# Softmax by head on ScalarE ahead of the transposes, and the layer norms on GpSimd, in an audio tower kernel

## The reference

```python
h = tokens(x)                       # 93 overlapping patches of 16 frames a sequence, 128 numbers each, + bias
h = h + attention(layernorm(h))     # a second layer norm with gamma and beta inside
h = h + experts(layernorm(h))
# attention, 8 heads of 64; q, k, v = projection, then 3 taps along the sequence
sim  = q @ k.T * 64 ** -0.5 - slope[head] * abs(i - j);  sim[j > i] = -max
out  = softmax(sim) @ v;  return out @ wout.T
# experts: 2 of 16 experts for each token; each expert's mean of silu(x @ w1.T) over its tokens goes through w2
```

## Time and profile before

| what | value |
|---|---|
| median of 3 runs | 793.95 us (793.44 to 796.95) |
| profiled execution | 798.25 us, span of its instructions 796.4 us |
| PE busy | 742.8 us, 93% of the span |
| DVE, ACT, POOL busy | 618.8, 471.6, 375.1 us (78%, 59%, 47%) |
| mean granted TensorE clock | 0.965 of 2.4 GHz |
| attention part (first to last row maximum) | 73.0 to 631.3 us |

### The profile page before, as it was taken

One profiled execution on the slowest core, in us unless ns is written; L12 is line 12 of the kernel. 1 busy time (PEld: TensorE's weight loads), 2 busy tenths in 40 slices (PEclk: granted clock), 3 DMA queues, 4 the chain that ended last, 5 costly groups with the idle time before them and its releaser, 6 DMA issues.

```text
span 796.4 us, 20698 instructions
## 1 busy us (share of the span) xinstructions
PE 742.8 (93%) x6770; PEld 691.7 (87%) x6770; DVE 618.8 (78%) x1645; ACT 471.6 (59%) x998; POOL 375.1 (47%) x390
## 2 busy tenths in 40 slices
PE   5678999999999999999999999998998878999986
PEld 4568999999999999999999999997877777999984
DVE  2255878888888888888888888889988648888875
ACT  3444556666566656666655656565543456899960
POOL 3642243666564655655565646554362455122200
PEclk9887999999999999999999999999999968999996
DMA  5421123331221111222111221102124012122205
GB/s 184 140 67 51 40 80 101 127 103 51 57 65 53 49 49 49 53 58 59 49 49 50 68 53 51 50 11 71 33 75 170 19 45 67 51 66 63 62 22 154
DMA packets 44269, 53.97 MB, mean 68 GB/s; under 512 B 13651, under 2 KB 31251, under 8 KB 43696
## 3 DMA queue, kind: packets, MB, share of 16 engines
q1 hardware_dynamic: 30048, 38.84, 16.9%
q0 software_dynamic: 12544, 12.87, 5.8%
q10 hardware_dynamic: 1616, 1.48, 0.6%
HBM read 42.69 MB, written 10.26 MB: 66 GB/s over the span
## 4 chain that ended last, share of the span: by engine, by line
PE 75%; DVE 12%; ACT 4%; issue 3%; DMA 2%; POOL 2%; DVEq 1%; ACTq 0%; SPq 0%
PE psTP L452 10%; PE psSO L590 9%; PE psTP L453 8%; PE psTP L454 8%; PE psSO L672 7%; PE psSO L612 6%; PE psSO L538 4%; PE psTP L524 3%; PE psTP L557 3%; PE psSO L710 3%; PE psTP L710 3%; DMA x_raw<-in_x 2%; PE psTP L635 2%; PE psSO L607 2%; DVE qkv L975 2%
## 5 line engine op out<-in xcount | busy, mean ns | idle before, releaser
L1329 POOL DMA_INDIRECT expert_rows<-hn,slot x128 | 167.6, 1309 | 66.6 <-DVE slot L1177 34.3
L1262 POOL TENSOR_TENSOR x_lo<-x_raw,x_hi 128x752 fp32r<-128x752 f32 x64 | 114.9, 1796 | 142.6 <-ACT x_hi L780 142.6
L975 DVE SCALAR_TENSOR_TENSOR qkv<-psTP,taps,qkv 128x368 f32<-128x368 f32 x192 | 113.9, 593 | 74.6 <-ACT qkv L788 73.2
L788 ACT ACTIVATE qkv<-psTP,taps 128x372 f32<-128x372 f32 x192 | 108.8, 567 | 89.0 <-PE psTP L454 88.7
L978 DVE SCALAR_TENSOR_TENSOR qkv<-psTP,taps,qkv 128x364 f32<-128x364 f32 x192 | 114.6, 597 | 6.8
L452 PE MATMUL psTP<-x_hi,wtok_hi 128*128 128x376 f32 x256 | 94.5, 369 | 13.7 <-DVE wtok_lo L963 9.0
L590 PEld LDWEIGHTS psSO<-vrow,probT 93*93 93x93 f32 x1024 | 94.6, 164 | 4.5 <-ACT probT L830 3.5
L590 PE MATMUL psSO<-vrow,probT 93*93 93x65 f32 x1024 | 95.0, 247 | 1.8 <-DVE resid L1110 0.8
L453 PE MATMUL psTP<-x_lo,wtok_hi 128*128 128x376 f32 x256 | 88.1, 344 | 0.0
L454 PE MATMUL psTP<-x_hi,wtok_lo 128*128 128x376 f32 x256 | 87.8, 343 | 0.0
L452 PE MATMUL psTP<-xnT_hi,wqkv_hi 128*128 128x372 f32 x192 | 77.8, 405 | 9.1 <-DVE qkv L978 5.0
(11 more groups left out here) (193 smaller groups left out, 1577.3 us busy)
## 6 DMA issues: line engine op xcount, KB each, us to landing
x_raw<-in_x SPq DMA_DIRECT2D x64, 376.0 KB, 3.2
w1s<-in_w POOLq DMA_DIRECT2D x8, 512.0 KB, 4.8
w<-in_w SPq DMA_DIRECT2D x4, 1024.0 KB, 6.9
out<-resid SPq DMA_DIRECT2D x16, 160.0 KB, 2.5
xsE<-expert_rows SPq DMA_DIRECT2D x36, 64.0 KB, 2.1
xs<-expert_rows SPq DMA_DIRECT2D x36, 64.0 KB, 1.8
xs<-expert_rows POOLq DMA_DIRECT2D x36, 64.0 KB, 2.1
expert_rows<-hn,slot POOLq DMA_INDIRECT x128, 3.5
```

Of the source, the lines that this page charges most:

```text
L788: nc.scalar.activation(qkv[u][:, k, :, :], psP[(k + 1) % 2][:, 0:GT].rearrange("p (b n) -> p b n", n=NT), ACT.Copy, scale=taps[:, k, 2:3]) ...
L975: nc.vector.scalar_tensor_tensor(dst[:, :, 1:NT], src[:, :, 0:NT - 1], taps[:, k, 1:2], dst[:, :, 1:NT], ALU.mult, ALU.add).then_inc(tap1_ ...
L1262: nc.gpsimd.tensor_tensor(x_lo[u][:, 0:PIECE], x_raw[u][:, :], x_hi[u][:, 0:PIECE].bitcast(F32), ALU.subtract)\
L1329: nc.gpsimd.indirect_dma_start(rows, bass.IndirectOffsetOnAxis(slot[1 - u][:, c:c + 1], 0), hn[1 - u][:, c % GB, :], None)\
```

## The change

The softmax is turned round. Before, the row maximum was subtracted, the scores were transposed, the exponential was taken on the way out of PSUM, and the sum and the division came behind the product with the values. Now:

- The scores are made negative (taps of q scaled by -1/8, bias with the other sign), DVE takes their minimum, and ACT's exponential reads them from PSUM with scale -1 and the minimum as bias, which is a number per partition and head: so there is one instruction for each head, 8 of 93x93, in two halves (exponentials(0) and (1)), with the copy of v between them.
- DVE sums prob, takes the reciprocal, and multiplies: three instructions behind a wait for both halves (exp_done), between the first conv and the other two of a step.
- PE transposes the finished probabilities into psPT (parts of psO's first bank and of psV), ACT copies them to probT, and the product has vrow as weights (93x64) and probT as moving data, so that its output is already transposed; head pairs lie on the two halves of the columns. The transposes of attn and the array attn are gone, and so are the ones in vrow.
- PE's order is: scores, first projection, transposes of prob, one patch tap, transposes of v, one tap, the product, second projection, a tap, a tap, third projection, output projection. ACT starts a step with the first tap2, the copy to resid and x_hi.
- Both layer norms' last part, ACT's four Identity instructions, becomes two instructions of GpSimd (93x512, product and sum), ahead of x_lo in its queue.

```diff
--- before.py
+++ after.py
-        vrow = [sb(f"vrow{u}", [NT, H, DH + 1]) for u in range(2)]
-        rmax = sb("rmax", [NT, 2, 4])
-        shifted = sb("shifted", [NT, 2, 4, NT])
+        vrow = [sb(f"vrow{u}", [NT, H, DH]) for u in range(2)]
+        rmin = sb("rmin", [NT, 2, 4])
+        prob = sb("prob", [NT, 2, 4, NT])
+        den = sb("den", [NT, 2, 4])
         probT = sb("probT", [NT, 2, 4, NT])
         rden = sb("rden", [NT, 2, 4])
-        attn = sb("attn", [NT, H * DH])
...
-        psTot = psO[:, 0, 264:264 + E]
+        psTot = psO[:, 1, 0:E]
         psRT = psV[:, 384:384 + NT]
+        psPT = [psO[:NT, 0, 0:GT], psV[:NT, 0:GT]]
...
+            def scores(t, u, s, n):
+
+                if s == 0:
+                    wait(pe, conv_done, (t - 3) * NBLK + 2 * QB)
+                    if isinstance(t, int) and t == 3:
+                        pe.wait_ge(bias_cast, 4)
+                        pe.wait_ge(attn_w_in, 16 * 4)
+                wait(pe, exp_done, n * 2)
+                wait(pe, rden_done, n)
+                for a in range(2):
+                    nc.tensor.matmul(psS[:NT, a, 0:4 * NT], ident16[:NT, :NT], bias[:, a, :],
+                                     start=True, stop=False, skip_group_check=True)
+                for hh in range(4):
+                    for a in range(2):
+                        lo = 64 * a
+                        mm = nc.tensor.matmul(psS[:NT, a, hh * NT:(hh + 1) * NT],
+                                              qkv[1 - u][lo:lo + 64, hh, s, :], qkv[1 - u][lo:lo + 64, QB + hh, s, :],
+                                              start=False, stop=True, skip_group_check=True)
+                mm.then_inc(s_mm, 1)
+
+            def turn_prob(t, f, s, n):
+
+                pe.wait_ge(prob_ready, n)
+                wait(pe, res_add, n - 1)
+                pe.wait_ge(v_evac, n)
+                if f.scat and s == 1:
+                    wait(pe, rwT_evac, t - 4)
+                for a in range(2):
+                    for hh in range(4):
+                        mm = nc.tensor.transpose(psPT[a][:, hh * NT:(hh + 1) * NT], prob[:, a, hh, :], ident[:NT, :NT])
+                    mm.then_inc(p_tr, 1)
+
+            def turn_values(t, u, f, s, n):
+
+                if s == 0:
+                    pe.wait_ge(conv_done, (t - 2) * NBLK)
+                wait(pe, p_evac, n * 2)
+                for j in range(QB):
+                    mm = nc.tensor.transpose(psV[:NT, j * 128:(j + 1) * 128],
+                                             qkv[1 - u][:, 2 * QB + j, s, :], ident[:, :])
+                mm.then_inc(v_tr, 1)
+
+            def weigh(s, n):
+
+                pe.wait_ge(p_evac, n * 2)
+                pe.wait_ge(v_evac, n)
+                for hh in range(4):
+                    for a in range(2):
+                        mm = nc.tensor.matmul(psO[64 * a:64 * a + 64, 0, hh * NT:(hh + 1) * NT],
+                                              vrow[(s + 1) % 2][:, 2 * hh + a, :], probT[:, a, hh, :],
+                                              start=True, stop=True)
+                mm.then_inc(pv_mm, 1)
...
+                    if f.attn:
+                        scores(t, u, s, n)
+                    if f.proj:
+                        proj(t, u, f, 3 * s)
                     if prev:
-
-                        pe.wait_ge(shift_done, n)
-                        for a in range(2):
-                            for hh in range(4):
-                                mm = nc.tensor.transpose(psS[:NT, a, hh * NT:(hh + 1) * NT], shifted[:, a, hh, :],
-                                                         ident[:NT, :NT])
-                            mm.then_inc(p_tr, 1)
+                        turn_prob(t, f, s, n)
...
+                        turn_values(t, u, f, s, n)
...
+                        weigh(s, n)
...
-                        pe.wait_ge(norm_done, n)
-                        for j in range(QB):
-                            mm = nc.tensor.transpose(psV[:, j * NT:(j + 1) * NT], attn[:, j * 128:(j + 1) * 128],
-                                                     ident[:NT, :NT])
-                        mm.then_inc(a_tr, 1)
...
-            def normalise(g, rstd, shift, dst, s_shift, s_done):
-
-                wait_apart(ac, s_shift, g + 1)
-                for b in range(GB):
-                    i = nc.scalar.activation(dst[:, b, :], resid[:, bass.ds(g * (GB * D) + b * D, D)], ACT.Identity,
-                                             bias=shift[:, b:b + 1], scale=rstd[:, b:b + 1])
-                i.then_inc(s_done, 1)
+            def exponentials(a):
+
+                for hh in range(4):
+                    i = nc.scalar.activation(prob[:, a, hh, :], psS[:NT, a, hh * NT:(hh + 1) * NT], ACT.Exp,
+                                             bias=rmin[:, a, hh:hh + 1], scale=-1.0)
+                i.then_inc(exp_done, 1)
...
+                    if f.proj:
+                        tap2(t, u, 3 * s)
+                    if f.norm and s == 0:
+
+                        wait(ac, tok_tr, t)
+                        nc.scalar.activation(resid[:, bass.ds((t - 1) * (GB * D), GB * D)], psP[0][:NT, :],
+                                             ACT.Copy).then_inc(res_evac, 1)
+                    if f.tok and f.more(t, s):
+                        ac.wait_ge(x_in[(s + 1) % 2], t * (16 * GB // 2) + (16 * ((s + 1) // 2) + 16))
+                        high(t * GB + (s + 1), (s + 1) % 2)
                     if prev:
                         wait(ac, pv_mm, n - 1)
                         for a in range(2):
                             ac.wait_ge(p_tr, n * 2 - 1 + a)
-                            nc.scalar.activation(probT[:, a, :, :].rearrange("p h n -> p (h n)"),
-                                                 psS[:NT, a, 0:4 * NT], ACT.Exp).then_inc(p_evac, 1)
+                            nc.scalar.activation(probT[:, a, :, :].rearrange("p h n -> p (h n)"), psPT[a],
+                                                 ACT.Copy).then_inc(p_evac, 1)
                     if f.gate and s == 2:
                         wait(ac, hnT_tr, t - 3)
                         nc.scalar.activation(hnT[:, :], psHn, ACT.Copy).then_inc(hnT_evac, 1)
                     if f.attn:
+                        ac.wait_ge(min_done, n + 1)
+                        wait(ac, p_tr, n * 2)
+                        exponentials(0)
                         ac.wait_ge(v_tr, n + 1)
                         wait(ac, pv_mm, n - 1)
-                        if isinstance(t, int) and t == 3 and s == 0:
-                            ac.wait_ge(vones_ready, 2)
-                        nc.scalar.activation(vrow[s % 2][:, :, 0:DH],
-                                             psV[:NT, :].rearrange("p (h d) -> p h d", d=DH), ACT.Copy)\
+                        nc.scalar.activation(vrow[s % 2][:, :, :].rearrange("p h d -> p (h d)"), psV[:NT, :], ACT.Copy)\
                             .then_inc(v_evac, 1)
                     if q == 0 or q == 1:
                         quad_copy(q)
-                    if f.proj:
-                        tap2(t, u, 3 * s)
-                    if f.norm and s == 0:
-
-                        wait(ac, tok_tr, t)
-                        nc.scalar.activation(resid[:, bass.ds((t - 1) * (GB * D), GB * D)], psP[0][:NT, :],
-                                             ACT.Copy).then_inc(res_evac, 1)
                     if f.norm and s == 3:
                         wait(ac, xnT_tr, t)
                         wait(ac, xnT_lo_done, t - 1)
@@ -856,26 +858,17 @@
                                              scale=gam[:, 0:1]).then_inc(xnT_evac, 1)
                         wait(ac, xnT_evac, t)
                         nc.scalar.activation(xnT_hi[1 - u][:, :], xnT[:, :], ACT.Copy).then_inc(xnT_hi_done, 1)
-                    if f.tok and f.more(t, s):
-                        ac.wait_ge(x_in[(s + 1) % 2], t * (16 * GB // 2) + (16 * ((s + 1) // 2) + 16))
-                        high(t * GB + (s + 1), (s + 1) % 2)
-                    if f.norm and s == 2:
-                        normalise(t - 1, rstd, shift, xn, ln_shift, xn_ready)
-                    if f.gate and s == 1:
-                        wait(ac, scattered[u], (t - u - 4) * (16 * GB))
-                        normalise(t - 4, rstd2, shift2, hn[u], ln2_shift, hn_ready)
+                    if f.attn:
+                        exponentials(1)
...
+                    if f.attn:
+                        dve.wait_ge(s_mm, n + 1)
+                        nc.vector.tensor_reduce(rmin[:, :, :], heads(psS, NT), AXX, ALU.min).then_inc(min_done, 1)
                     if f.proj:
                         conv(t, u, 3 * s)
-                    if prev:
-                        o = heads(psO, DH + 1)
-                        dve.wait_ge(pv_mm, n)
-                        nc.vector.reciprocal(rden[:, :, :], o[:, :, :, DH]).then_inc(den_done, 1)
-                        dve.wait_ge(den_done, n)
```

(33 more changed lines are left out.)

121 lines of the change are left out of this document (36 added, 85 removed).

## The result

The changed kernel takes **929.75 us** (median of 4 runs, 922.79 to 932.15) against 795.45 of before in the same session (4 runs, 793.44 to 797.93): ratio 1.1672, 95% interval [1.1598, 1.1747]. It is 134 us slower. The forecast was 900 with a range of 850 to 945, so the sign and the range hold and the forecast lies 30 us low. The profiled execution took 932.15 us.

The account below looks back on a forecast made before the run. TensorE's bound was to pass to a round trip through VectorE and ACT: 41.7 us a full group plus 2.2 for port meetings, 673 us in all against 567, +106, giving 900 us; range 850 to 945.

Parts of the forecast that it names:

- the ring: Round trip from res_add through minimum, exponentials, sum, product and taps to res_add: extras + 8.22 us, no step shorter.
- s = 1 and s = 2: Second and third steps of a four-step group, with layer-norm statistics: 9.7 us each, plus 1.1 for the meeting on the port.
- the exponential: Each of ACT's eight 93x93 exponentials: 0.34 us long, 0.25 from start to start, bounds 0.15 and 0.39.
- the meeting on the port: VectorE's product prob x rden starts inside GpSimd's x_lo and comes 1.1 us late in two steps, 2.2 per full group.
- s = 3: Last step of a four-step group, with route, choose and ACT's xnT copies between the exponentials' halves: 11.8 us.
- rival 1: The ring without the meetings on the port, x_lo elsewhere or the wait short: 28 us less, 872; chance 0.25.
- idles the rest: TensorE needs 33.4 to 35.2 us of a 41.7 us group and only idles for the remainder.
- rival 2: Longer ring: exponentials at 0.39 us (972), or TensorE's clock falling in one step of every second group (936); chance 0.17.
- s = 0: First step of a four-step group, where ACT's copies delay the first exponential to 3.2 us: 10.4 us.
- the wait of turn_values for the probT copies falls into that idle time: TensorE's transposes of v wait for the probT copies, as psPT lies in psV's bank; hidden in TensorE's idle time.
- rival 3: TensorE stays the bound and the kernel gets faster: 743 to 772 us, say 760; chance 0.09.
- my low bound: TensorE's product with the values, sixteen passes paired on column halves: 0.83 us, as for the scores product, against 1.30.

Follow-up runs that it names:

- e2: Changed kernel plus a spare 0.68 us VectorE reduction in each step, ahead of the wait for the exponentials: 936.19 us, ratio 1.1744.
- e3: Changed kernel plus a spare 0.68 us VectorE reduction in each step, behind the product prob x rden: 954.28 us, ratio 1.1973.
- e1: Changed kernel with the reciprocal rden in PSUM instead of SBUF, the next scores waiting for the product: 889.87 us, ratio 1.1196.
- e6: Changed kernel with both layer norms' last part back on ACT, behind the second half of the exponentials: 887.71 us, ratio 1.1155.
- e5: Changed kernel with two exponentials of 93x372 for eight of 93x93, the minimum computed but not subtracted: 893.23 us, ratio 1.1222.
- e4: Kernel before the change plus a spare 0.68 us VectorE reduction in each step, behind the subtraction shifted: 819.09 us, ratio 1.0289.
- e11: Changed kernel with rden in PSUM and two exponentials of 93x372 that leave the minimum out: 850.67 us, ratio 1.0691.
- e12: Changed kernel with rden in PSUM, VectorE's extras behind the minimum, ACT's copies reordered, two exponentials without the minimum: 809.35 us, ratio 1.0167.
- e13: The kernel of e12 without the reduction for the minimum, the exponentials waiting for the scores alone: 802.75 us, ratio 1.008.

## Why the prediction was right, and where it was off

**Right: the ring.** That PE stops being the bound and that DVE waits at the sum in every step came true (64 waits, 139.0 us), and e2 against e3 shows the place: work ahead of the wait is nearly free, work behind it is paid. s = 1 and s = 2 came out at 10.92 and 10.70 for 10.8.

**Right: the exponential.** Mean 341 ns, four in 1.01 us, for 0.34 and 0.25 apart (it was 0.22). The way from the first to the sum took 2.43 us for 2.63.

**Right in mechanism, small in size: the meeting on the port.** I gave it 1.1 us in two steps; it measured 1.29 and 1.52, and 32 us over the kernel for my 28. What the sum left out is that VectorE's small instructions with two SBUF inputs are caught as well: the 0.14 us difference in s = 3 cost 1.15 more. Removing the product's meetings gave 40 us (e1), removing all of them 42 (e6). So rival 1, which left the meetings out at 872, is refuted: 58 us below the measurement, and the product's line shows them. The Trainium skill (SBUF — State Buffer, SBUF: two separate sides) says that a VectorE instruction with two SBUF inputs and a GpSimd instruction that reads SBUF hold the shared ports exclusively for a whole instruction, and that the other fully blocks; this trace agrees for a single meeting (the product, 0.93 us alone, ended 0.8 us behind x_lo). In e5 the product did not get its turn between two GpSimd instructions that follow without a gap, and lasted 3.50 us.

**The largest step that failed: that PE merely "idles the rest".** PE was busy 38.28 us of 46.15 (83%, I said 76 to 80), because part of it ran at 1.2 GHz. I had the fall of the clock in rival 2, as whole steps in every second group, and left it out of the forecast because before stood at 1.00. What happened is smaller and more frequent: it follows waits of 1.8 to 2.4 us, reaches the ring through a late output projection, late scores and a late projection, and costs 2.0 us in s = 0 of six groups in eleven and up to 0.57 in s = 3. e4 shows the same in the kernel before. Where it doesn't strike, s = 0 takes 10.8 for the forecast 10.4: the first exponential starts 3.8 us behind the end of res_add for my 3.2, since PE has its first projection in front of the transposes of prob, which I left out:

```profile
424.53 0.44 PE L454 MATMUL psTP<-xnT_hi,wqkv_hi 128*128 128x372 f32 x1
...
428.48 1.02 ACT L800 ACTIVATE prob<-psSO,rmin 93x93 f32<-93x93 f32 x4
```

**The step that was harmless here and is not elsewhere: "the wait of turn_values for the probT copies falls into that idle time".** In after it does, and costs only through the clock. But it is a second bound right under the ring, which e11, e12 and e13 ran into, and my rival 3 ("faster", at 760) had overlooked it: with the ring out of the way the kernel still needs 37.2 us a group. The saving on PE that rival 3 rests on is real: the product with the values starts at 394.40 and the next matmul at 395.19 in after, 0.79 us at full clock, just under my low bound of 0.83 and 0.5 less than the 1.30 of the earlier trace rows.

**GpSimd.** The norm's two instructions took 1.04 us each for 1.28; x_lo's 1.80 was as before; POOL's load in a group rose by 5.2 us, as said, but by luck: the norms' four instructions make 4.2 of it, and the rest is that the eight indirect DMAs took 11.5 us for 10.5.

The sum of a group, corrected from the table: 10.83 + 10.92 + 10.70 + 13.09 = 45.5 for the faster kind, 12.8 + 10.92 + 10.70 + 13.15 = 47.6 for the slower, for my 43.9. In s = 0 that is 0.4 more than forecast and 2.0 in six groups of eleven, 1.5 in the mean; in s = 3 up to 1.3 (the small difference and the half clock); s = 1 and s = 2 are as forecast. The eleven groups' mean, the first still short, is 46.4, which makes 12 x 2.5 = 30 us more than the forecast. Of the 2.5, about 1.4 is the lower clock (1.1 in s = 0, 0.3 in s = 3), 0.8 the caught difference in s = 3 less what other terms there gave back, 0.4 the late first exponential.

That the twelve groups alone make up the 30 us is partly luck. The row minimum's line starts from 65.5 to 764.2 us, 140 us more than the 558.3 of the earlier trace rows and not 104 (63 of 64 intervals of my +106): the four short groups were longer too, by some 7 us. The minimum also starts 7.5 us earlier than the maximum did, where I had taken nothing:

```profile
L1072 DVE TENSOR_REDUCE rmin<-psSO x64: 892/920/930, 65.5 to 764.2; 93x8 f32<-93x744 f32 x64
```

## What to carry to other kernels

When an engine's queue is strict, price a change by walking the round trip it creates, from the instruction behind which the next step starts back to itself, over every engine, and list who else's copy stands between its halves; a shorter operation in a round trip gives only what the next wait in it allows. Keep VectorE instructions with two SBUF inputs away from GpSimd work, or put one input in PSUM, and then look which instruction is caught next: in e1 it was another one. When a bound falls, look for the next one before counting the gain: here five limits lay behind each other (port, extras, ACT's order, exponentials, a shared PSUM bank), the saving on TensorE lay under all of them, and undoing the first four won back 127 of 134 us only with the minimum left out.

## What the runs showed of the hardware

- A VectorE instruction of 93x4 values with two SBUF inputs took 1.29 us instead of 0.14, issued inside a GpSimd instruction of 1.79 us; one of 93x64 took 1.69 instead of 0.22 inside one of 1.84 (e1); one of 93x744 took 3.50 instead of 0.93 against two GpSimd instructions in a row. The last with one input in PSUM: 924 to 926 ns in all 64 cases.
- TensorE waits of 1.76 to 2.40 us were followed by 3 to 6 us at 1.2 GHz in after and e4, though not each time: of two waits of 1.81 and 1.82 us at the same place, one was and one was not. Waits of 0.9 us in e13 were not; the clock stood at 1.00 over its group. In e4 a group with one such wait took 41.0 us for 36.8.
- Sixteen matmuls with 64 weight columns, in pairs on the two halves of the columns, took 0.79 us from start to next start, against 1.30 for sixteen with 93 weight columns and 65 moving ones in the kernel before.
- A GpSimd product or sum of 93x512 float32 took 1.04 us, while one of 128x752 with an fp32r result took 1.80.
